# One semaphore for both copies of the transposed probabilities, and a wait for keys moved ahead of the output projection

## The reference, cut to what matters

```python
x = layer_norm(image_embeds)            # 77 context rows
l = layer_norm(latents)                 # 256 rows
q = l @ Wq
kv = concatenate([x, l], axis=1) @ Wkv  # 333 keys and values
w = softmax(q k^T * scale)              # per head
out = (w v) @ Wo
x = x + tanh(g_xattn) * out
x = x + tanh(g_ffn) * experts(_layernorm(x))
```

## Time and profile before

| | |
|---|---|
| median of 3 runs | 1275.37 us (1272.56 to 1277.68) |
| the profiled execution | 1275.89 us, of which the span of instructions 1274.2 us |
| PE busy | 1224.4 us, 96% of the span |
| DVE, ACT, POOL busy | 880.6, 762.7 and 459.2 us |
| mean granted clock of TensorE | 0.992 |

### The profile page before, as it was taken

How to read it: one execution, slowest core, us unless ns; L and a number is a source line. 1 busy time by engine, 2 the same in 40 slices (tenths; PEclk the granted TensorE clock), 3 DMA queues, 4 the chain that set the end, 5 groups by cost and what they waited for, 6 DMA issues and landing times.

```text
span 1274.2 us, 28111 instructions
## 1 busy us (share of the span) xinstructions
PE 1224.4 (96%) x8922; PEld 1008.9 (79%) x8922; DVE 880.6 (69%) x2643; ACT 762.7 (60%) x2231; POOL 459.2 (36%) x638
## 2 busy tenths in 40 slices
PE   5999999999999999999999999999999999999995
PEld 5788888888887888788878887888888878787774
DVE  6667777777777777777767776777776666334564
ACT  5676666666666666666656665666666644344442
POOL 4222323333333333233323333333332323355564
PEclk9999999999999999999999999999999999999998
DMA  9900000000000000000000000000000163436676
GB/s 288 319 23 2 1 13 1 29 1 29 3 28 3 29 2 29 3 29 2 29 3 29 2 29 3 29 2 29 1 26 1 59 219 100 122 121 203 204 236 212
DMA packets 68496, 79.29 MB, mean 62 GB/s; under 512 B 7585, under 2 KB 60785, under 8 KB 68337
## 3 DMA queue, kind: packets, MB, share of 16 engines
q1 hardware_dynamic: 60472, 56.18, 14.8%
q0 software_dynamic: 6912, 18.95, 4.0%
q10 hardware_dynamic: 952, 2.18, 0.5%
HBM read 39.38 MB, written 37.90 MB: 61 GB/s over the span
## 4 chain that ended last, share of the span: by engine, by line
PE 58%; issue 25%; POOL 11%; DVE 4%; DMA 1%; ACT 1%; POOLq 0%; DVEq 0%; SPq 0%; ACTq 0%
PE pj L1390 16%; PE ov L1379 8%; PE st L1436 6%; PE st L1420 6%; PE st L536 6%; POOL probs L1091 4%; PE yb L1499 4%; PE pj L489 3%; PE ov L555 3%; POOL slots_x L962 2%; POOL probs L1088 2%; PE st L526 2%; PE yb L503 1%; PE pj L492 1%; POOL rstd L1071 1%
## 5 line engine op out<-in xcount | busy, mean ns | idle before, releaser
L1159 ACT ACTIVATE probs<-st,neg_max 128x333 f32<-128x333 f32 x512 | 268.9, 539 | 265.5 <-DVE neg_max L1319 241.4
L1088 POOL TENSOR_TENSOR probs<-probs,inv_sum 128x333 f32<-128x333 f32 x128 | 94.8, 740 | 652.9 <-DVE inv_sum L1331 652.9
L1319 DVE TENSOR_REDUCE neg_max<-st 128x2 f32<-128x666 f32 x256 | 206.5, 846 | 126.2 <-PE st L1436 125.2
L1379 PE MATMUL ov<-PT,V 128*64 128x256 f32 (+1 forms) x1536 | 197.4, 392 | 0.1
L1420 PE MATMUL st<-ident,probs 128*128 128x128 f32 (+1 forms) x1536 | 189.0, 272 | 1.4 <-ACT probs L1159 1.4
L1420 PEld LDWEIGHTS st<-ident,probs 128*128 128x128 f32 (+1 forms) x1536 | 176.1, 143 | 5.0 <-issue 1.8
L1436 PE MATMUL st<-K_hl,Q_hl 64*128 64x334 f32 x1536 | 152.2, 330 | 14.7 <-issue 10.5
L1354 DVE COPY PT<-st 128x512 f32<-128x512 f32 x256 | 163.7, 681 | 0.0
L1390 PE MATMUL pj<-wkv,lT 128*128 128x512 f32 (+1 forms) x576 | 156.9, 407 | 3.3 <-DVE wkv L1282 1.6
L1379 PEld LDWEIGHTS ov<-PT,V 128*64 128x64 f32 (+1 forms) x1536 | 100.2, 138 | 64.3 <-issue 28.0
L1091 POOL TENSOR_SCALAR probs<-probs,inv_sum 128x333 f32<-128x333 f32 x128 | 144.5, 1129 | 0.0
(11 more groups left out here) (178 smaller groups left out, 1754.1 us busy)
## 6 DMA issues: line engine op xcount, KB each, us to landing
slots_x<-zeros SPq DMA_DIRECT2D x10, 1032.0 KB, 13.4
V<-slots_x SPq DMA_DIRECT2D x80, 129.0 KB
yg<-routed_y SPq DMA_DIRECT2D x32, 256.0 KB
h_kept<-h_turned SPq DMA_DIRECT2D x16, 256.0 KB
hT<-h_kept SPq DMA_DIRECT2D x16, 256.0 KB, 3.3
out<-X SPq DMA_DIRECT2D x32, 128.0 KB
X<-in_x SPq DMA_DIRECT2D x2, 1024.0 KB, 13.6
w_gu<-in_L_ffn_expert_gate_w SPq DMA_DIRECT2D x2, 960.0 KB, 8.0
```

What stands on the lines that cost most here:

```text
L1088: pool.tensor_tensor(probs[:, v, 0, 0:SKV], probs[:, v, 0, 0:SKV], inv_sum[:, v, 0:1].to_broadcast([P, SKV]), ALU.mult).then_inc(normed, 1)
L1159: nc.scalar.activation(probs[:, v, i, 0:SKV], st_bank(i)[:, 0:SKV], ACT.Exp, bias=neg_max[:, v, i:i + 1], accum_out=sums[:, v, i:i + 1]).t ...
L1319: nc.vector.tensor_reduce(neg_max[:, v, 2 * i:2 * i + 2], st[i][:, :, 0:SKV], AX.X, ALU.max, negate=True).then_inc(maxed, 1)
L1379: last = nc.tensor.matmul(ov[half * HALF:(half + 1) * HALF, 0:SQ], V[0:kn, kt, head * DH:(head + 1) * DH], PT[0:kn, v, kt, half * SQ:(half ...
```

## The change

DVE's and ACT's copies of transposed probabilities now raise one semaphore, `pt_read`, three times a pair. The scores wait for it once, `NKT` being 3. The scores' wait for K's low half (`pj_free`) is gone; in its place PE waits for K of the same step ahead of the output projection. `head_outputs` no longer waits for `ot_lo` and for the copies, except in the last steps, where no scores are left (`has(LAG_S)` is false).

```diff
@@ scalar @@
-                copy(PT[0:kn, v, 2, :], st_bank(2)[0:kn, :], ACT.Copy).then_inc(pt_hi, 1)
+                copy(PT[0:kn, v, 2, :], st_bank(2)[0:kn, :], ACT.Copy).then_inc(pt_read, 1)
@@ vector @@
-                    nc.vector.tensor_copy(PT[:, v, kt, :], st_bank(kt)).then_inc(pt_lo, 1)
+                    nc.vector.tensor_copy(PT[:, v, kt, :], st_bank(kt)).then_inc(pt_read, 1)
@@ head_outputs @@
-        if known(m):
+        if not has(LAG_S):
             pe.wait_ge(ot_lo, m)
...
-        pe.wait_ge(pt_lo, 2 * m + 2)
-        pe.wait_ge(pt_hi, m + 1)
+        if not has(LAG_S):
+            pe.wait_ge(pt_read, NKT * (m + 1))
@@ tensor, step @@
                 m, r = PAIRS * bb + u - LAG_S, (u - LAG_S) % 2
-                _, _, kfree, kvalue = filled("K", PAIRS, bb, u - LAG_S)
-                pe.wait_ge(kfree, kvalue + 1)
...
                 if known(m - 1):
-                    pe.wait_ge(pt_lo, 2 * (m - 1))
-                    pe.wait_ge(pt_hi, m - 1)
+                    pe.wait_ge(pt_read, NKT * (m - 1))
...
             route_tensor(pe, bb, u, has)
+            if has(0):
+                _, _, kfree, kvalue = filled("K", PAIRS, bb, u)
+                pe.wait_ge(kfree, kvalue + 1)
             if has(LAG_Y):
```

More of the change, by code:

```diff
@@ L515, in first_tiles @@
             pe.wait_ge(att.exped, 4 * att.N)
-            pe.wait_ge(att.pt_lo, 2 * att.N)
-            pe.wait_ge(att.pt_hi, att.N)
+            pe.wait_ge(att.pt_read, 3 * att.N)
         def tile(i):
@@ L701, in attention @@
     pt_full = sem("pt_full")
-    pt_lo = sem("pt_lo")
-    pt_hi = sem("pt_hi")
+    pt_read = sem("pt_read")
     ov_full = sem("ov_full")
@@ L1414, in turned @@
                 elif kt == 0:
-                    pe.wait_ge(pt_lo, 2 * m)
-                    pe.wait_ge(pt_hi, m)
+                    pe.wait_ge(pt_read, NKT * m)
                 for i in range(4):
@@ L1531, in attention @@
         last_step=PAIRS * (B - 1) + SECOND, pj_free=pj_free,
-        pj_full=pj_full, ov_full=ov_full, y_full=y_full, y_read=y_read, exped=exped, pt_lo=pt_lo, pt_hi=pt_hi,
+        pj_full=pj_full, ov_full=ov_full, y_full=y_full, y_read=y_read, exped=exped, pt_read=pt_read,
         ot_lo=ot_lo, h_rows=h_rows, slots_clear=slots_clear)
```

## The result

The changed kernel takes 1280.93 us (median of 8 runs, 1278.75 to 1281.83), the one before 1275.28 us in the same measurement (8 runs, 1272.56 to 1277.75). The ratio is estimated at 1.0035, 95% interval 1.0024 to 1.0047 (the two medians divide to 1.0044): slower, by less than the 0.5% that counted as no change. The median is 4.3 us above the forecast of 1276.6 and 0.4 above the upper end of the range in us. The medians differ by 5.7 us. The profiled execution has a span of 1279.1 us, 4.9 more than before; these 4.9 us are what has to be found.

The account below looks back on a forecast made before the run. PE, busy 1224.4 of 1274.2 us, was taken as the bound; -0.6 (waits), +1.4 (jump) and +0.4 (clock) gave +1.2 us on the profiled 1275.89, so 1277.1, a median of 1276.6 us; 8-in-10 range 1272 to 1280.5.

Parts of the forecast that it names:

- Waits that go: PE's sequencer: dropped waits ahead of outputs give nothing; ahead of scores they matter only where copies are late; -0.6 us.
- late scores: Scores in steps without values, where DVE's copies come late: 0.045 us gained for each of 13, -0.6 us.
- The wait for keys ahead of the projection: Output projection in steps without values: slips 0.02 to 0.06 us, hidden by the scores' idle time; costs nothing.
- The jump: Loop's end on PE: K's wait starts each of four taken jumps 0.60 us later, landing gains 0.24; +1.4 us.
- The first rival: Loop's end: K's wait does not hold the sequencer, each jump gains 0.24; median 1273.8 us, chance 0.13.
- The clock: Behind the jumps: longer idle time may put the fourth at a lower clock too; a quarter of 1.55, +0.4 us.
- DVE, ACT and POOL keep their instructions; the expert stage is untouched: Other engines and expert stage: no term of their own in the sum.
- the rival with a second stall: Loop re-entries: shifted landing makes PE wait for the next code piece too, 10.5 us; 1288 us, chance 0.05.

Follow-up runs that it names:

- e6: Changed kernel with all of PE's steps written out in full, so no loop or jump on PE; 1264.41 us.
- e7: Changed kernel with PE's steps written out, and keys awaited only in the first two steps with scores only; 1264.13 us.
- e11: Kernel before the change with PE's steps written out and 128 more instructions at PE's start; 1277.38 us.
- e5: Changed kernel with one more wait at a trip's end, for copies of transposed probabilities, holding the jump 1.2 us longer; 1288.00 us.
- e9: Changed kernel with keys awaited only in the first two steps with scores only, and 60 semaphore increments at PE's start; 1275.11 us.
- e4: Changed kernel with 48 semaphore increments that nobody waits for at PE's start, moving all later code; 1277.15 us.
- e12: Changed kernel with 48 semaphore increments behind PE's first transposes, where it waits for rows anyway; 1279.15 us.

## Why the prediction was right or wrong, step by step

- **Waits that go.** Right. The 128 waits ahead of the outputs and the keys' wait at the scores were free in the steps, as e6, e7 and e11 show. The late scores came 0.05 us earlier 12 or 13 times, about -0.6 as forecast.
- **The wait for keys ahead of the projection.** Right: covered by the scores' own wait; e6 and e7 differ by 0.3 us. (In the steps without values and routing the projection slips by 0.11 us against the matmuls ahead of it, not by the 0.02 to 0.06 worked out, and the scores still come earlier.)
- **The jump.** Right in its mechanism, mis-sized. 0.60 later and 0.22 nearer to the score, as worked out (0.60 and 0.24); but the jumps took 3.76 us instead of 3.63, which I had taken as fixed. So +0.51 for each, +2.0 instead of +1.4 from score to score. Over all profiles with a loop taken jumps last 3.27 to 4.03 us; what sets that stays open. The first rival, by which the sequencer is not held, had the jumps start ahead of K's end. None did in the changed kernel, and e5 moved them by the 1.2 us of its wait. The Trainium skill, page "Perfetto Trace Analysis", section "Tensor Engine Instruction (MATMUL, LD_WEIGHTS)", which puts the semaphore wait into a queue behind the sequencer, does not agree with these jumps. (A queue too short for the projection's instructions that stand between the wait and the jump would look the same; no run tells the two apart.)
- **The clock.** Right in sign: +0.4 forecast, +0.8 found, from start to start of the first 60 matmuls behind the four landings: +1.1 from one stretch of 3.4 us more behind the fourth, -0.3 behind the others. Idle time alone does not decide it: a jump with 3.24 us of idle time was followed by full clock in the changed kernel, and one with 2.20 by half clock in e9.
- **The step that failed: "DVE, ACT and POOL keep their instructions; the expert stage is untouched", hence nothing else.** I saw that the code ahead of the loop got shorter, and used it only for the landing (the rival with a second stall, which did not occur). The same shift moves each load of PE's code against the work of other engines. Here six scatters instead of four met one, and the idle time ahead of the logits rose by 1.35 us. e4 and e9 took it away by moving code alone.
- **The end.** From the last output projection on, the changed kernel takes 228.4 us and the one before 227.3. Over all 14 profiles this stage takes 227.3 to 228.7 us, with no tie that I found to the waits or to the loads. These 1.2 us stay open.

The sum in the profile: -0.6 late scores, +2.0 jumps, +0.8 clock, +1.35 logits, +1.2 at the end, 4.75 of 4.9 us. Of the 3.7 us by which this exceeds the forecast, 1.0 was mis-sized, 1.35 is the missing term, and 1.2 is unexplained.

## What to carry to other kernels

In a long program on PE, count what an edit does to the place of all later code, not only the instructions that go: look up the instruction queue's packets in the trace and see which transfers lie within a microsecond of them, since a few instructions more or fewer can be worth as much as the edit itself. Undoing half an edit is then no clean test; run each version at a second offset of the code, and take what the padding costs at the start from the trace. And keep waits away from the end of a loop: what the last matmul waits for there delays the jump one for one, while the same wait in a step that is ahead of its data costs nothing; where the code may grow, no jump at all was worth 11 us here.

## What the runs showed of the hardware

- One 16 KB load of code next to an indirect DMA made it 1.3 us later (3.26 after 1.92 us, medians of 52 and 144). One or two of a scatter's 16 parts are late (the fourteenth comes at 1.88 us, the last at 3.24), which fits my reading that the load holds up the packets on one DMA engine; the traces don't name the engine. The Trainium skill, page "Runtime: NRT & Kernel Launch", section "Instruction fetch mechanics", calls the cost of going from one such block to the next mostly hidden. In e6, whose steps are all written out, no matmul waits for "issue", which agrees; the cost comes by way of DVE.
- Code written out in full brought no stall of PE within the steps: e6 loads 74 packets of code for its 17,844 matmuls and weight loads, against 83 with the loop, and has no "issue" wait among the scores.
- An instruction on PE that only raises a semaphore shows 51 ns in the trace, but in all five kernels with such instructions one starts every 0.15 us. 24 of them at the start (0.9 to 4.4 us) are hidden, since PE's first matmul waits until 5.7 us anyway; with 48 it starts at 8.3, with 60 at 10.2, with 128 at 20.6. In e12 48 of them take 7.2 us, and a wait of 3.25 us hides only a part.
